# Moving a convolution's first unit, a last stage's first tiles and one addition between engines in a decoder layer

## The reference

```python
x = x + attention(layernorm(x))              # 32 query heads, 8 key heads, window of 128, sinks
x = x + ssm_conv(ctx, ctx, layernorm(x))     # below, 32 heads of 8 rows each
x = x + layernorm(x) @ sum(factors) / sqrt(8) + bias

kv  = einsum('bhil,bhjl->bijhl', k_, v_)     # k = v = ctx, so kv[i,j] == kv[j,i]
y   = causal convolution of kv with ssm_kernel along l (512 long), by FFT
out = einsum('bijhl,bhil->bjhl', y + kv * D, q_)
```

## Time and profile before

| | |
|---|---|
| median of 3 runs | 2010.59 us (2010.47 to 2011.04) |
| the profiled execution | 2011.53 us, span 2009.7 us |
| TensorE busy | 1952.0 us |
| VectorE busy | 1577.7 us |
| ScalarE busy | 932.4 us |
| GpSimd busy | 782.2 us |

### The profile page before, as it was taken

How to read it: one execution, slowest core, us unless ns; L and a number is a source line. 1 busy time by engine, 2 the same in 40 slices (tenths; PEclk the granted TensorE clock), 3 DMA queues, 4 the chain that set the end, 5 groups by cost and what they waited for, 6 DMA issues and landing times.

```text
span 2009.7 us, 44848 instructions
## 1 busy us (share of the span) xinstructions
PE 1952.0 (97%) x15500; PEld 1602.5 (80%) x15500; DVE 1577.7 (79%) x5012; ACT 932.4 (46%) x3481; POOL 782.2 (39%) x883
## 2 busy tenths in 40 slices
PE   6899999999999999999999999999998999999899
PEld 6788888888888888888888888888876777777687
DVE  6777777777777777877777777777776999999887
ACT  4545554555555455555555555455553222222333
POOL 3444343343333333433333333333322454554454
PEclk8999999999999999999999999999999999999999
DMA  6146111111211122211111111112123533333343
GB/s 213 43 121 145 62 55 63 54 54 54 75 54 53 44 98 108 70 44 53 54 54 54 64 54 54 54 66 82 34 83 137 168 91 84 92 86 89 98 146 121
DMA packets 71538, 162.20 MB, mean 81 GB/s; under 512 B 6656, under 2 KB 15232, under 8 KB 71184
## 3 DMA queue, kind: packets, MB, share of 16 engines
q1 hardware_dynamic: 62720, 142.48, 21.4%
q0 software_dynamic: 3840, 8.39, 2.3%
q10 hardware_dynamic: 4752, 8.46, 1.1%
HBM read 108.96 MB, written 50.41 MB: 79 GB/s over the span
## 4 chain that ended last, share of the span: by engine, by line
PE 83%; DVE 11%; issue 2%; ACT 2%; POOL 1%; DMA 0%; DVEq 0%; ACTq 0%; POOLq 0%
PE banks L528 22%; PE banks L590 18%; PE banks L567 9%; PE banks L543 9%; PE banks L1138 8%; PE banks L553 6%; PE banks L521 4%; PE banks L1344 4%; DVE terms L1170 2%; DVE banks L1184 2%; DVE banks L1180 1%; DVE terms L1187 1%; PE banks L478 1%; ACT pr L664 1%; DVE banks L1190 1%
## 5 line engine op out<-in xcount | busy, mean ns | idle before, releaser
L664 ACT ACTIVATE pr<-pr,mx 128x128 f32<-128x128 f32 x1024 | 399.0, 391 | 352.8 <-DVE mx L882 352.8
L743 POOL TENSOR_TENSOR m<-m,rope_sb 128x512 f32<-128x512 f32 x160 | 206.4, 1290 | 513.7 <-ACT m L651 513.7
L528 PE MATMUL banks<-xTh,wh 128*128 128x256 f32 x1280 | 376.9, 294 | 2.5 <-DVE xTl L842 1.4
L528 PE MATMUL banks<-xTl,wh 128*128 128x256 f32 x1280 | 363.6, 284 | 0.0
L528 PE MATMUL banks<-xTh,wl 128*128 128x256 f32 x1280 | 363.1, 284 | 0.0
L1138 PE MATMUL banks<-kv,tap 128*128 128x288 f32 x1280 | 323.9, 410 | 12.7 <-DVE res L1194 10.9
L1138 PEld LDWEIGHTS banks<-kv,tap 128*128 128x128 f32 x1280 | 238.1, 190 | 98.1 <-issue 36.5
L528 PEld LDWEIGHTS banks<-xTh,wh 128*128 128x128 f32 x1280 | 246.8, 193 | 4.3 <-issue 1.9
L891 DVE TENSOR_TENSOR den<-ac,es 128x4 f32<-128x4 f32 x256 | 51.2, 200 | 253.3 <-ACT es L667 253.2
L528 PEld LDWEIGHTS banks<-xTl,wh 128*128 128x128 f32 x1280 | 247.1, 193 | 0.0
L528 PEld LDWEIGHTS banks<-xTh,wl 128*128 128x128 f32 x1280 | 246.6, 193 | 0.0
(11 more groups left out here) (110 smaller groups left out, 3854.3 us busy)
## 6 DMA issues: line engine op xcount, KB each, us to landing
tap<-padded_taps SPq DMA_DIRECT2D x64, 256.0 KB, 3.3
kk<-in_ctxt SPq DMA_DIRECT2D x64, 192.0 KB, 3.5
x_in<-in_x SPq DMA_DIRECT2D x16, 512.0 KB, 3.9
xt_split<-xTh SPq DMA_DIRECT2D x16, 512.0 KB, 2.6
xt_split<-xTl SPq DMA_DIRECT2D x16, 512.0 KB, 3.6
xb<-in_x SPq DMA_DIRECT2D x16, 512.0 KB, 4.6
factors<-in_factors POOLq DMA_DIRECT2D x8, 1024.0 KB, 8.8
x_part_rows<-x SPq DMA_DIRECT2D x16, 512.0 KB, 3.1
```

Of the source, the lines that this page charges most:

```text
L528: last = pe.matmul(bank[:, h * T:(h + 1) * T], w[:, n, c, h * P:(h + 1) * P], a[:, s, c, :], start=(c == 0 and i == 0), stop=(c == KD - 1 ...
L664: act.activation(pr[:, s, a, cols], pr[:, s, a, cols], ACT.Exp, bias=mx[:, s, i:i + 1], scale=-1.0, accum_out=ac[:, s, i:i + 1])
L743: pool.tensor_tensor(m2[:, s], m2[:, s], rope_sb[:, 1 if i == 0 else 0, 1:3], ALU.mult).then_inc(sin_ready, 1)
```

## The change

1. In attention's drain, GpSimd makes the pairs of units 0 and 1 behind p = 2 and 3 instead of 5 and 6. ScalarE fetches the queries of units 0 and 1 behind p = 4 (ahead of the factors' high parts) and 6 instead of 6 and 7. TensorE issues unit 0's products at p = 3, j = 1, ahead of the last batch's first projection part, and VectorE unit 0's multiplications and first three additions at p = 5, j = 1, ahead of the residual. The second x1 transposes of the second half come at p = 5, j = 1 instead of p = 6, j = 0.
2. Behind the drain TensorE issues unit 1's products, and then the last two x1 transposes, now into banks 2 and 3. Unit 1's last column waits for the last residual, unit 2's third and fourth for the copies of the transposes. SP issues the loads of unit 2 and the contexts of unit 3 before the last store of transposed x1.
3. The last addition of each unit goes from VectorE to GpSimd, behind the pairs of unit u + 2. The third addition writes SBUF instead of PSUM. Products wait for one_added instead of res_ready.
4. The products of a unit go column by column instead of tap block by tap block.
5. VectorE does unit 63's multiplications, then the fronts of the last stage's tiles 0 and 1, then unit 63's three additions, then the low part of tile 0, then the front of tile 2. GpSimd's addition for unit 63 comes behind tile 1's bias, ScalarE's placement behind tile 0's high part.

```diff
@@ attention, tensor @@
+                    if y.drain and p == 3 and j == 1:
+                        conv.first_products(pe)
                     for s in parts_of(y, p, j):
                         out_projection(y, p, s)
         bodies(body)
-        conv.first_products(pe)
+        conv.second_products(pe)
+        pe.wait_ge(one_added, 1)
         for t in range(NT):
-            x1_transposes(2 * B - 1, t, (QM + 1) * 2 * B)
+            x1_transposes(2 * B - 1, t, None, sP[:, 2 + t])
@@ attention, sync @@
         bodies(body)
+        conv.more_loads(sp)
         sp.wait_ge(x1t_evac, 2 * B)
@@ attention, scalar @@
+                if y.drain and p in (4, 6):
+                    conv.first_queries(act, p // 2 - 2)
                 if y.drain and p == 4:
                     mix.factors_high(act)
-                if y.drain and p in (6, 7):
-                    conv.first_queries(act, p - 6)
@@ attention, gpsimd @@
-                if y.drain and p in (5, 6):
-                    conv.first_pairs(pool, p - 5)
+                if y.drain and p in (2, 3):
+                    conv.first_pairs(pool, p - 2)
@@ attention, vector @@
+                    if y.drain and p == 5 and j == 1:
+                        conv.first_sums(dve)
                     if residual_tile(y, p, j) is not None:
@@ attention @@
+    X1_AT = {2: 0, 4: 1}
+    X1_LAST = {2: 0, 3: 1}
     def x1_here(y, p, j):
-        return p % 4 in (1, 2) and j == 0 and late(y, 3, p)
+        tiles = X1_LAST if y.drain and p >= 4 else X1_AT
+        return tiles.get(2 * (p % 4) + j) if late(y, 3, p) else None
@@ convolution @@
+    def more_loads(sp):
+        load(sp, 2)
+        load_contexts(sp, 3)
     def sync(sp):
-        for u in range(2, NCU):
+        load_taps(sp, 3)
+        for u in range(4, NCU):
             load(sp, u)
+    def last_sum(pool, u):
+        n, s = CD * BG, u % 2
+        pool.wait_ge(one_added, u + 1)
+        wait(pool, res_placed, u - 1)
+        pool.tensor_tensor(res[:, s], terms[:, s, :, n:2 * n], terms[:, s, :, 2 * n:3 * n], ALU.add).then_inc(res_ready, 1)
     def gpsimd(pool):
-        for u in range(2, NCU):
-            pairs(pool, u)
+        for u in range(NCU):
+            if u + 2 < NCU:
+                pairs(pool, u + 2)
+            if u < NCU - 1:
+                last_sum(pool, u)
     def products(pe, u):
-        wait(pe, res_ready, u - 1)
-        for d in range(KD):
-            for c in range(d, KD):
+        wait(pe, one_added, u - 1)
+        for c in range(KD):
+            if u == 1 and c == KD - 1:
+                pe.wait_ge(x1_ready, 2 * NV)
+            if u == 2 and c == 2:
+                pe.wait_ge(x1t_evac, 2 * B)
+            for d in range(c + 1):
                 last = pe.matmul(y[:, s, c, 0:NY], tap[:, s, d * P:(d + 1) * P], kv[:, s, c - d, :],
                                  start=(d == 0), stop=(d == c))
+    def second_products(pe):
+        pe.wait_ge(x1t_evac, 2 * B - 2)
+        pe.wait_ge(pt_masked, 8 * NV)
+        pe.wait_ge(ot_lo, 8 * NV)
+        products(pe, 1)
@@ convolution, vector: unit_terms (the multiplications), unit_sums @@
-            dve.tensor_tensor(y[:, s, :, 3 * n:4 * n], tt[:, :, 0:n], y[:, s, :, 2 * n:3 * n],
-                              ALU.add).then_inc(one_added, 1)
-            dve.wait_ge(one_added, u + 1)
-            wait(dve, res_placed, u - 1)
-            dve.tensor_tensor(res[:, s], tt[:, :, n:2 * n], y[:, s, :, 3 * n:4 * n], ALU.add).then_inc(res_ready, 1)
+        dve.tensor_tensor(tt[:, :, 2 * n:3 * n], tt[:, :, 0:n], y[:, s, :, 2 * n:3 * n],
+                          ALU.add).then_inc(one_added, 1)
+        for u in range(1, NCU - 1):
+            unit_terms(dve, u)
+            unit_sums(dve, u)
+        unit_terms(dve, NCU - 1)
@@ last stage, scalar / gpsimd / vector @@
+            if v == 2:
+                conv.last_place(act)
+            if v == 1:
+                conv.last_result(pool)
+            if v == 2:
+                conv.last_sums(dve)
+                low(0)
             if has(v, 0):
+                front(v)
```

More of the change, by code:

```diff
@@ L469, in x_transposes, with x1_transposes @@
             last.then_inc(xt_done, 1)
-        def x1_transposes(r, t, roped):
+        def x1_transposes(r, t, roped, bank=wP):
             n = 2 * (r - B) + t
             pe.wait_ge(x1n_ready, n + 1)
-            pe.wait_ge(m_ready, roped)
-            wait(pe, x1t_evac, n)
+            if roped is not None:
+                pe.wait_ge(m_ready, roped)
+                wait(pe, x1t_evac, n)
             for c in range(KD):
-                last = pe.transpose(wP[:, c * P:(c + 1) * P], x1n[:, t, c * P:(c + 1) * P], id_sb[:])
+                last = pe.transpose(bank[:, c * P:(c + 1) * P], x1n[:, t, c * P:(c + 1) * P], id_sb[:])
             last.then_inc(x1t_done, 1)
@@ L680, in o_high, with x1_evac @@
             act.copy(oTh[:, (u // 4) % 2, c], vP[:, 0:T]).then_inc(ot_hi, 1)
[L682 removed]
+        def x1_evac(r, t, bank=wP):
             n = 2 * (r - B) + t
@@ L1011, in conv_part @@
 def conv_part(nc, ctx, space, ctx_in, pad_dram, q2_dram, x1t_stored, qk_done, v_done, m_ready, sin_ready, v_ready, qr_ready,
-              masked, pt_masked, ot_lo, out_done, x1_ready, x1t_evac, tap_out, res_ready, res_placed):
+              masked, pt_masked, ot_lo, out_done, x1_ready, x1t_evac, tap_out, one_added, res_ready, res_placed):
     def sem(name):
@@ L1050, in projected, with load_contexts @@
         eng.wait_ge(v_done, NV)
-    def load(sp, u):
+    def load_contexts(sp, u):
         bg, h, s = where(u)
@@ L1055, in load, with load_taps @@
         sp.dma_start(kk[:, s], ctx_in[bg, h]).then_inc(kk_landed[s], 16)
+    def load_taps(sp, u):
+        bg, h, s = where(u)
         wait(sp, conv_done, u - 1)
@@ L1058, in load @@
           .then_inc(tap_landed[s], 16)
+    def load(sp, u):
+        load_contexts(sp, u)
+        load_taps(sp, u)
     def load_queries(sp, b):
@@ L1128, in scalar, with last_place @@
                 fetch(act, u + 1)
-            place(act, u)
+            if u < NCU - 1:
+                place(act, u)
+    def last_place(act):
+        place(act, NCU - 1)
     def products(pe, u):
@@ L1201, in mix_part @@
+    return Conv(first_loads, more_loads, first_pairs, first_queries, first_products, second_products, first_sums,
+                last_sums, last_result, last_place, sync, tensor, scalar, gpsimd, vector)
+def mix_part(nc, ctx, space, conv, x1_dram, bias, out, x1_stored, out_done, qk_done, qr_ready, f_in, one_added, res_placed):
     NV = B * NT
@@ L1323, in tensor @@
                 if v < 2:
-                    pe.wait_ge(res_ready, NBG * CH - 1)
+                    pe.wait_ge(one_added, NBG * CH - 1)
                 pe.wait_ge(res_placed, CH * (b // BG + 1))
@@ L1339, in tensor @@
                     pe.wait_ge(f_lo, KD)
-                    pe.wait_ge(res_ready, NBG * CH)
+                    pe.wait_ge(one_added, NBG * CH)
                 wait(pe, fin_ready, v - 4)
@@ L1402, in decoder_layer @@
         tap_out = sem("tap_out")
+        one_added = sem("one_added")
         res_ready = sem("res_ready")
```

142 lines of the change are left out of this document (77 added, 65 removed).

## The result

The changed kernel takes 1990.93 us (median of 4 runs, 1990.33 to 1992.66), the one before 2010.82 on the same chip (4 runs, 2010.47 to 2012.34). The ratio is 0.9899, with a 95% interval of 0.9887 to 0.9912: faster by 1.0%, clear of the noise. Forecast were 1990.4 us and a range of 1985.5 to 1996.5. The profiled execution took 1991.15, its span 1989.3, that is 20.4 less than before.

The account below looks back on a forecast made before the run. A two-unit loop of latencies between TensorE and VectorE, no full engine, was taken to bound the convolution. 13.5 + 5.2 + 1.5 = 20.2 us saved gave 1990.4 us against the median 2010.59; range 1985.5 to 1996.5.

Parts of the forecast that it names:

- The steady units: Convolution units: releasing 0.45 us earlier shortens a unit from 5.24 to 5.01 us, 13.5 us over 60 units.
- the loop: Convolution: TensorE's weight load, VectorE's multiplication and PSUM release, next load two units on; 10.47 us before, 10.02 forecast.
- The addition on GpSimd: Each unit's last addition, 256 elements, costs GpSimd 0.72 us; later pairs finish with 1.4 us of cover.
- rival 3: Convolution: GpSimd's in-order queue becomes the loop; kernel slower if the addition takes 3.2 us or more; chance of slower 0.04.
- The joint before: Attention's drain into the convolution: reordered work brings unit 3's first multiplication 5.2 us earlier.
- D(1): Start of VectorE's first multiplication of convolution unit 1, forecast at 1547.9.
- D(3): Start of VectorE's first multiplication of unit 3, forecast at 1560.6 against 1565.76 before.
- Unit 2's wait: Convolution's start: unit 2 becomes late because its contexts are issued behind the store of x1, at about 1544.1.
- P(2): Start of unit 2's first weight load on TensorE, forecast at 1550.6.
- The joint behind: Convolution into the last stage: tiles' fronts ahead of unit 63's additions save 1.5 us, bounds 0.5 and 2.5.
- D(63): Start of VectorE's first multiplication of unit 63, the last convolution unit; forecast near 1861, 1880.27 before.
- Rival 1: Convolution: late tap loads become the wait, 0.3 to 0.8 us in eight units or 5.1 throughout; 1993 to 1996; chance 0.16.

Follow-up runs that it names:

- experiment 1: Changed kernel with one wait put back: a unit's products wait for res_ready (GpSimd's addition) instead of one_added; 2016.16 us, ratio 1.0024 to the kernel before.
- experiment 6: Changed kernel with three more 256-element additions on GpSimd in each unit, written to a buffer nothing reads; 2011.59 us, ratio 1.0001 to the kernel before.
- experiment 2: Changed kernel with each unit's last addition back on VectorE, products still waiting for one_added; 1995.71 us, ratio 0.9924 to the kernel before.
- experiment 9: Kernel before with only the early release (one_added), the third sum in terms and the last addition on GpSimd; 1997.48 us, ratio 0.9931.
- experiment 7: Changed kernel with VectorE's first multiplication split: three banks when their products are done, the fourth at the unit's end; 1980.28 us, ratio 0.9845 to the kernel before.
- experiment 8: Changed kernel with unit 1's pairs moved back behind p = 5 of the drain; 1990.99 us (one run).
- experiment 10: Changed kernel with SP issuing unit 2's loads before it waits for the last residual, not behind it; 1990.73 us, ratio 0.9898 to the kernel before.
- experiment 3: Changed kernel with unit 63 finished as a whole before the last stage's first tile, as before the change; 1992.66 us, ratio 0.9905 to the kernel before.

## Why the prediction was right

The forecast missed the median by 0.5 us. A part of that closeness is luck: the runs of the kernel before are spread over 1.9 us, and in the profiled executions of the changed kernel and of experiments 1 and 6, whose work up to there is the same, the drain's first normalisation starts at 1529.2, 1527.6 and 1529.5. The mechanism stands on more than that. Term by term:

- **The steady units.** 13.5 forecast, 13.4 measured, 5.02 a unit instead of 5.01. Experiments 1, 2 and 9 show that the cause is the place of the release. Experiment 7 shows that what was left of the loop was latency: with a split first multiplication the unit went from 5.02 to 4.85 and the work of a unit stayed the same.
- **The addition on GpSimd.** 0.72 forecast, 0.73 measured. The pairs that end at 1704.22 stand behind unit u's sum and are those of unit u + 3, whose weight load starts at 1705.76: a cover of 1.5 us, for 1.4 forecast. VectorE's first multiplication also waits for GpSimd's sum of two units before (`wait(dve, res_ready, u - 1)`), which the prediction doesn't name; that sum ends at 1701.59 and the multiplication starts at 1706.16, so it never held. But rival 3 had the wrong law: GpSimd's full queue sets 5.36 with three more additions (experiment 6), where the chain of waits gave 5.21 to 5.24.
- **The joint before.** 5.2 forecast, 5.3 measured; D(1) 1548.09 for 1547.9, D(3) 1560.44 for 1560.6. Counted from the last PV product, which comes 0.26 later in the trace after (1524.69 for 1524.43), the joint gives 5.6: the wait for unit 2 is 0.5 shorter than forecast. The normalisation went as read: L834 is 0.55 without the pairs and 2.46 with them (experiment 8). Pairs beside attention did slow one small VectorE instruction from 0.16 to 0.69 us, L900 above, which lay on no path.
- **Unit 2's wait.** P(2) was forecast at 1550.6 and came at 1550.37. What the prediction didn't see is that this wait keeps unit 2's pairs off the last normalisations (experiment 10).
- **The joint behind.** 1.5 forecast, 1.7 by the traces of before and after (23.5 against 21.9 behind D(63)). The chain of the last stage's start:

```profile
1871.05 3.97 PE banks L1408 x12
...
1875.90 3.06 PE banks L1408 x12
...
1879.83 2.74 PE banks L1408 x12
...
1883.45 2.77 PE banks L1408 x12
```

The first product comes 9.5 behind D(63), the fourth block 21.9 (forecast 9.6 and 22.0), against 23.5 before. The first block takes 3.97 us instead of some 2.75, which the prediction didn't have. It cost next to nothing, because the second block waits for the low half of tile 1, which ends at 1875.84:

```profile
1875.15 0.69 DVE L1430 TENSOR_TENSOR nTl<-banks,nTh 128x512 fp32r<-128x512 f32 x1 [0.29 <-ACT nTh L1342]
```

- **Rival 1, late loads.** It did not come. The taps of the query stretch land in 4.0 us (median of nine, at most 4.2). The prediction's 4.5 came from a single tap, the slowest of the nine in the trace before, whose median is 4.1. The list of waits from 1560 to 1860 has none of TensorE's for a tap (engine, tile and line, releaser, us in all, times, longest):

```profile
PEld banks L1180 <- issue: 21.4, 60, 0.5
DVE terms L1214 <- PE banks L1180: 21.1, 60, 0.5
```

The margin was 0.7 instead of 0.2, and 0.5 for the slowest. The later units do run with half the traffic: in the trace before, 178 GB/s from 1565 to 1585 and 81 from 1700 to 1720. The rows show what is left of the loop: TensorE and VectorE each wait for the other, 21 us each.

## What to carry to other kernels

Here two engines hand two buffers to and fro and neither is full (4.84 and 5.04 of 5.24 us), and the period was half of the loop of latencies: 5.24 with a loop of 10.47, 5.02 with 10.04. In such a case find the release that closes the loop, move it to the last reader of the buffer (13.4 us here), and let the consumer start on the parts that are complete (10.6 us, experiment 7). Price an engine that takes over work by its wait chain and by the sum of its queue, and take the larger: in experiment 6 the chain gave 5.21 to 5.24 a unit, and the full queue set 5.36. When an earlier transfer brings nothing, look at what it set free, and beside which instruction that now runs: in experiment 10 two normalisations went from 1.00 to 3.04 us.

## What the hardware showed that was not expected

- An addition of VectorE's with two SBUF inputs and its normalisation ended 0.3 behind GpSimd's pairs, if the pairs had begun first or with them. The addition went from 0.42 to 2.51 us with the same start, and ended 0.28 behind (experiment 2). The normalisation, which began 0.08 behind the pairs, went from 0.55 to 2.46, and ended 0.29 behind (experiment 8); two normalisations of 1.00 together, begun 0.07 behind, became 3.04 (experiment 10). L900, of four elements a partition, took 0.69 instead of 0.16, and ended 0.03 behind the pairs. It went the other way too: pairs that started at 1520.09, 0.11 behind a VectorE multiplication of SBUF operands (L905), took 2.72 instead of 2.25. Not every instruction in SBUF is held: the statistics (L822, one SBUF input) took 0.68 at 1521.54, beside these pairs, and 0.68 to 0.70 in all their 32 places. VectorE's first multiplication, with a PSUM input and 1024 elements, takes 1.22 to 1.23 in all 64 units, beside GpSimd's pairs too. By which mechanism one engine holds up the other is not shown.
- TensorE's granted clock fell to 0.50 at the start of the last stage. Windows of the changed kernel: length, then busy time of PE, PEld, DVE, ACT, POOL, granted clock, DMA share, GB/s.

```profile
1862.50:1864.50 2.00, 0.03 (x1) 0.00 (x0) 2.00 (x5) 0.43 (x1) 0.00 (x0) 1.00 0.00 0
1864.50:1870.00 5.50, 2.74 (x13) 2.13 (x14) 4.91 (x13) 1.82 (x3) 3.71 (x6) 0.66 0.30 98
...
1871.00:1873.00 2.00, 1.95 (x5) 1.56 (x6) 1.79 (x6) 0.62 (x1) 0.02 (x1) 0.50 0.00 0
1873.30:1875.00 1.70, 1.70 (x10) 1.35 (x9) 1.35 (x5) 1.17 (x2) 1.62 (x3) 1.00 0.20 28
```

TensorE had stood nearly still for two microseconds (0.03 busy), and was busy for 0.63 of the next 2.5, at whose end the granted clock was 0.50 (0.85 on the mean of 1864.5 to 1867). From 1868 on it was busy nearly without a gap (2.94 of the 3.00 to 1871, the clock at 0.50). The first products of the block then run at 0.50 of the clock, one each 0.43 us, and at 1.00 from 1873.3 on, one each 0.23. The kernel before shows the same, 0.50 from 1888 to 1892.8, so the change did not bring it; what differs is how much of the first block falls into it (experiment 3). What brings the clock down and up again is not shown by a run.
